# Warm products of 128 columns, expert weights rounded later, and an earlier finish of a tile, in a conditioned mixture-of-experts block

## What is computed

```
h  = einsum('bct,bcd->bdt', x, table[conditions])        # 4096 rows of 256
u  = square(relu(h @ up_w))                              # 256 -> 1024
m  = (h @ expert_weight) * top_2(h @ gate_w).sum()       # 256 -> 256, one scale per row
y  = u @ down_w + m                                      # 1024 -> 256
out = x + (y - mean(y)) * rsqrt(var(y) + 1e-5) * gamma + beta
```

## Time and profile before

| what | value |
|---|---|
| median of 3 runs (lowest, highest) | 230.84 us (230.8, 231.0) |
| the profiled execution's own time | 230.09 us |
| its span, first to last instruction | 228.5 us |
| TensorE busy with products, with weight loads | 221.8 us (97%), 191.9 us (84%) |
| VectorE, ScalarE, GpSimd busy | 162.2, 105.7, 130.5 us |
| granted TensorE clock over the span | 1.00 |
| stores of the last block's tiles | 4 of 128 KB, 1.7 us from issue to landing |

### The profile page before, as it was taken

One profiled execution on the slowest core, in us unless ns is written; L12 is line 12 of the kernel. 1 busy time (PEld: TensorE's weight loads), 2 busy tenths in 40 slices (PEclk: granted clock), 3 DMA queues, 4 the chain that ended last, 5 costly groups with the idle time before them and its releaser, 6 DMA issues.

```text
span 228.5 us, 3998 instructions
## 1 busy us (share of the span) xinstructions
PE 221.8 (97%) x1260; PEld 191.9 (84%) x1260; DVE 162.2 (71%) x352; ACT 105.7 (46%) x187; POOL 130.5 (57%) x131
## 2 busy tenths in 40 slices
PE   7999999999999999999999999999999999999992
PEld 2888888988898888888888888888888888888892
DVE  6486975877667877667677766587766766777884
ACT  3378944444455355444545435534454444444000
POOL 3748776575536663656555664366555575557411
PEclk9999999999999999999999999999999999999999
DMA  3867123030503011000200002000020002000021
GB/s 98 239 205 227 41 68 102 8 99 7 185 11 98 9 43 53 0 0 3 92 0 0 3 0 95 0 3 0 0 95 1 0 0 71 25 0 0 19 99 69
DMA packets 17177, 11.81 MB, mean 52 GB/s; under 512 B 6660, under 2 KB 16900, under 8 KB 17156
## 3 DMA queue, kind: packets, MB, share of 16 engines
q1 hardware_dynamic: 15460, 10.43, 15.2%
q10 hardware_dynamic: 1280, 1.07, 1.5%
q0 software_dynamic: 416, 0.05, 0.2%
HBM read 7.35 MB, written 4.19 MB: 51 GB/s over the span
## 4 chain that ended last, share of the span: by engine, by line
PE 93%; DVE 2%; DMA 1%; issue 1%; ACTq 1%; ACT 0%; DVEq 0%
PE up_ps L337 38%; PE down_ps L431 25%; PE down_ps L433 13%; PE hid_ps L303 5%; PE moe_ps L447 3%; PE moe_ps L449 3%; PE moe_ps L448 3%; DMA wd<-in_L_cond_weights_dram 1%; ACTq L513 1%; PE down_ps L303 1%; DVE up_lo L619 1%; DMA cond_row<-in_itok_B_dram 1%; PE down_ps L429 0%; PE down_ps L427 0%; PE down_ps L428 0%
## 5 line engine op out<-in xcount | busy, mean ns | idle before, releaser
L677 POOL TENSOR_TENSOR sq_lo<-square,sq_hi 128x512 fp32r<-128x512 f32 x64 | 83.6, 1310 | 78.6 <-DVE square L552 77.4
L431 PE MATMUL down_ps<-down_hl,sq_hi 128*128 128x512 f32 x248 | 88.8, 393 | 0.0
L433 PE MATMUL down_ps<-down_hl,sq_lo 128*128 128x256 f32 x248 | 69.6, 280 | 0.0
L552 DVE SCALAR_TENSOR_TENSOR square<-up_ps,relu 128x512 f32<-128x512 f32 x64 | 43.8, 686 | 35.7 <-ACT relu L491 26.2
L431 PEld LDWEIGHTS down_ps<-down_hl,sq_hi 128*128 128x128 f32 x248 | 46.5, 188 | 10.8 <-issue 0.3
L491 ACT ACTIVATE relu<-up_ps 128x512 f32<-128x512 f32 x64 | 38.1, 595 | 33.5 <-PE up_ps L337 33.5
L337 PE MATMUL up_ps<-hid_hi,up_hi 128*128 128x512 f32 (+1 forms) x136 | 52.8, 391 | 0.7 <-ACT hid_hi L476 0.3
L337 PE MATMUL up_ps<-hid_hi,up_lo 128*128 128x512 f32 (+1 forms) x136 | 51.1, 379 | 0.0
L433 PEld LDWEIGHTS down_ps<-down_hl,sq_lo 128*128 128x128 f32 x248 | 46.7, 188 | 2.4
L493 ACT ACTIVATE sq_hi<-relu 128x512 fp32r<-128x512 f32 x64 | 40.5, 633 | 2.0
L337 PE MATMUL up_ps<-hid_lo,up_hi 128*128 128x512 f32 (+1 forms) x136 | 40.6, 381 | 0.0
(11 more groups left out here) (62 smaller groups left out, 195.6 us busy)
## 6 DMA issues: line engine op xcount, KB each, us to landing
x_sb<-in_x_dram SPq DMA_DIRECT2D x7, 512.0 KB, 4.3
out_dram<-result SPq DMA_DIRECT2D x7, 512.0 KB, 3.1
wd<-in_L_cond_weights_dram SPq DMA_DIRECT2D x111, 4.0 KB, 1.6
x_sb<-in_L_ffn_down_w_dram SPq DMA_DIRECT2D x2, 512.0 KB, 4.4
x_sb<-in_x_dram ACTq DMA_DIRECT2D x2, 256.0 KB, 3.0
result<-in_L_ffn_up_w_dram ACTq DMA_DIRECT2D x2, 256.0 KB, 2.9
result<-in_L_ffn_up_w_dram SPq DMA_DIRECT2D x1, 512.0 KB, 4.6
out_dram<-result SPq DMA_DIRECT2D x4, 128.0 KB, 1.7
```

Of the source, the lines that this page charges most:

```text
L431: pe.matmul(dst[:, :], a_hi, down_hl[:, c, :, :].rearrange("p s t -> p (s t)"), start=(c == 0), stop=False)
L433: mm = pe.matmul(dst[:, T:2 * T], a_lo, down_hl[:, c, 0, :], start=False, stop=(c == CH - 1))
L552: dve.scalar_tensor_tensor(square[:, c % 2, :], up_ps[c % UPB][:, :], 0.0, relu[:, c % 2, :], ALU.max, ALU.mult).then_inc(square_done, 1)
L677: pool.tensor_tensor(sq_lo[:, j % 2, c, :], square[:, c % 2, :], sq_hi[:, j % 2, c, :].bitcast(f32), ALU.subtract).then_inc(sq_lo_done, 1)
```

## The change

Three things are changed. The warm products become 42 products of 128 columns, whose operands are both the program's constant one; the tile `warm`, its fill and the wait for it go. The rounding of the expert and gate weights moves on ACT behind `rectify(0, 0)`, and its low part on DVE behind `square_up(0, 0)`. In the last block, tile 2 is finished right behind tile 1, ahead of the work on tile 3.

```
-WARM = 10
+WARM = 42
...
-            pe.wait_ge(warm_ready, 1)
+            one = nc.const_aps.tensor(1.0, [P, P], bf16)
             for _ in range(WARM):
-                pe.matmul(up_ps[0][:, :], warm[:, 0:P], warm[:, :], start=True, stop=True)
+                pe.matmul(up_ps[0][:, 0:P], one, one, start=True, stop=True)
...
             hidden_first(1, 1)                                      # ACT
-            act.wait_ge(eg_landed, 32)
-            act.activation(eg_hi[:, :, :], eg_raw[:, :, :], ACT.Copy).then_inc(eg_hi_ready, 1)
...
                     rectify(j, c)
+                    if j == 0 and c == 0:
+                        act.wait_ge(eg_landed, 32)
+                        act.activation(eg_hi[:, :, :], eg_raw[:, :, :], ACT.Copy).then_inc(eg_hi_ready, 1)
...
-            dve.memset(warm[:, :], 1.0).then_inc(warm_ready, 1)
...
             split_up(2)                                             # DVE
-            dve.wait_ge(eg_hi_ready, 1)
-            dve.tensor_tensor(eg_lo[:, :, :], eg_raw[:, :, :], eg_hi[:, :, :].bitcast(f32), ALU.subtract) \
-                .then_inc(eg_lo_ready, 1)
...
                         square_up(j, c)
+                    if j == 0 and c == 0:
+                        dve.wait_ge(eg_hi_ready, 1)
+                        dve.tensor_tensor(eg_lo[:, :, :], eg_raw[:, :, :], eg_hi[:, :, :].bitcast(f32), ALU.subtract) \
+                            .then_inc(eg_lo_ready, 1)
...
                         if block < BLOCKS - 1:
                             finish(block, t)
-                        elif t > 0:
+                        elif 0 < t < TILES - 1:
                             finish(block, t - 1)
+                            if t == TILES - 2:
+                                finish(block, t)
```

More of the change, by code:

```diff
@@ L70, in adaln_ffn @@
         table_loaded = sb("table_loaded", [P, 1])
-        warm = sb("warm", [P, 512], bf16)
         hid_hi = sb("hid_hi", [P, 2, K, TOK], f32r)
@@ L120, in adaln_ffn @@
         result_moved = [sem("result_moved_even"), sem("result_moved_odd")]
-        warm_ready, consts_ready = map(sem, ("warm_ready", "consts_ready"))
+        consts_ready = sem("consts_ready")
         wd_zeroed = [sem("wd_zeroed_block0"), sem("wd_zeroed_rest")]
```

## The result

The changed kernel is slower: 231.18 us at the median of 9 runs (230.28 to 231.79) against 230.80 for the kernel before (9 runs, 230.11 to 231.0). The ratio is 1.0032, 95% interval 1.002 to 1.0045; the ratios here are worked out from the single times and are not the quotients of the medians. I had forecast 230.2.

What follows compares the result with a forecast made beforehand. PE's stream was taken as the bound (93% of the chain of waits). Gains of 0 + 0.48 + 0.10 + 0.05 = 0.63 us from the median 230.84 gave 230.2 us, own range 230.0 to 230.4, with rivals 229.5 to 230.9.

Steps and rivals of the forecast that it cites:

- The warm part is thus worth 0 to the end: Start: 42 products at 0.11 us end at 5.7, hidden because group 1's matrix holds PE until 6.80; gain 0.
- Rival 2: Start: weight loads pace the small warm products at 0.22 us each, 2.0 us late; time 232.2; chance 7%.
- the pace of 0.162: Start: load-and-product pairs at the lower clock, 0.162 us each, would end the warm products at 7.9, 1.5 past the cover.
- SP waits for none of the moved work, so this stays: Block 1's conditioning: SP's last matrix still lands at 16.57, leaving 0.48 us of the 0.56 gained.
- The expert weights, 0.48 us: Chunk 0's square comes earlier, PE's wait before 14.99 goes, and 0.48 us reaches the end; bounds 0 to 0.56.
- From then on PE doesn't wait in either trace: After block 1's conditioning, from about 16.6 us: no new PE wait, so the 0.48 us gain is kept.
- Hidden, with 0.8 to spare: eg_lo on DVE, 14.4 to 15.1 us, is ready 0.8 us before PE's expert products at 15.9.
- The finish: Tail: last finish starts 0.65 us after POOL's power, gaining 0.10; the last store running alone gains 0.05.
- Rival 1: Block 1's matrices land 0.3 us later and decide; total gain 0.15 to 0.4, time 230.6; chance 17%.
- Rival 3: Clock rises later, 1.5 to 2 us into the dense stretch from 7.86; 0.75 to 1.0 lost, net 231.2; 5%.
- Rival 4: Start 0.54 us earlier brings the clock's rise forward, some 0.5 to 0.7 us on top; 229.6; chance 9%.

Runs made afterwards that it cites:

- warm_only: Kernel before with only the warm products changed to 42 of 128 columns on the constant one; 231.51 against 230.44 us, ratio 1.0040.
- experts_only: Kernel before with only the rounding of the expert weights moved; 230.74 against 230.44 us, ratio 1.0006.
- finish_only: Kernel before with only tile 2 of the last block finished earlier; 230.35 against 230.44 us, ratio 0.9997.
- all_10x512_pool_waits: Whole change, but ten warm products of 512 columns on the constant one, and POOL's first sq_lo waits for eg_lo; 230.39 against 230.41 us, ratio 1.0004.
- const_10x512: Kernel before with its ten 512-column warm products on the constant one, without the fill; 230.42 against 230.41 us, ratio 0.9999.
- all_gate: all_10x512_pool_waits with DVE's gate for block 0's tile 2 moved ahead of squares 8 and 9; 230.27 against 230.37 us for the kernel before, ratio 1.0013.
- const_84x64: Kernel before with 84 warm products of 64 columns on the constant one; 231.65 against 230.44 us, ratio 1.0075.
- const_32x160: Kernel before with 32 warm products of 160 columns on the constant one; 230.32 against 230.44 us, ratio 1.0003.

## Why the prediction was wrong

- **The step that failed:** "The warm part is thus worth 0 to the end". Its own working held: 0.107 us a product against my 0.11, the matrix of group 1 at 6.67 against 6.80, no cost up to 7.86. But I counted the added instructions as columns and not as instructions. They cost 1.07 us at the median (warm_only), by a way that none of my rivals had: the fetch at 13.7 instead of 21.5 us, SP's issue of 1.45 instead of 0.42, the down weights' landing at 18.96 instead of 17.57, ACT, the expert products at 32.66 instead of 31.62. That the place of the fetch is the cause rests on these traces and on the table of widths, with the open ends said there. Rival 2, pacing by the weight loads, was of the right sign for the wrong reason; the 0.107 us refutes it, and with it the pace of 0.162 that I had scaled from the 81 ns of the Trainium skill, "TensorE: Matmul & The Clock Gate", section "Back-to-back issue gap".
- **"SP waits for none of the moved work, so this stays":** no semaphore, but SP's issue itself took 1.0 us longer (of the down weights in the profile after, of a matrix of block 1 in warm_only).
- **The expert weights, 0.48 us:** with this part the wait for the square went in eight of nine traces, and chunk 4 began at 14.5 to 14.9 in seven of them, 0.1 to 0.5 earlier (at 15.13, with 0.2 of the wait left, where the up weights landed late, and at 15.97 where the clock had fallen). "From then on PE doesn't wait in either trace" was the false sentence. A view that shows no wait doesn't show the slack. It was 0.16 us at 31.6 and less than nothing at 39.7, where the view of PE's weight loads of the kernel before already has a wait for ACT's scaled result (0.3 us) that I didn't use. DVE, ACT and POOL set the time of block 0 and 1, and the moved work stayed in their stream.
- **"Hidden, with 0.8 to spare":** I looked at when eg_lo is needed and not at who runs beside it. It moved from a place where POOL idled to one 0.05 to 0.25 us from POOL's first operation, and in experts_only PE did wait 0.3 us for it.
- **The finish:** start 0.65 behind POOL's power and 0.1 gained, as worked out; from there to the span's end 2.7 us instead of 2.8, within the 0 to 0.1 of the store. By itself (finish_only) the part isn't told apart from nothing.
- **Rival 1**, the matrices of block 1: they held PE in all_10x512_pool_waits and for up to 0.2 us after, but decided nothing, since the later waits were the tighter ones. **Rival 3**, a later clock, didn't show in the profile after (products of 256 columns 0.12 us apart from 7.92 on); a clock that fell again did in other kernels, see the last section. **Rival 4** didn't show: the same median in eleven runs of const_10x512, which starts just as early.
- **The median that I subtracted from** (230.84, three runs) was itself 0.4 us above what the kernel before showed later. Had the whole gain come, the time would have been near 229.8, and not the 230.2 of the forecast.

## What to carry to other kernels

Count added instructions also as bytes to be fetched, and look where in the DMA view the fetches of the engine stand: a piece that moves into a burst of loads can hold up the engine that issues them. Before crediting a removed wait to the end, walk PE's later semaphores and subtract, for each, the producer's end from the consumer's start; the smallest difference is all that can be gained. Work that is moved between two engines has a neighbour on the other engine, too.

## What the hardware showed unexpectedly

- The first fetch of 16 KB of instructions took 1.06 us of one DMA engine (1.0 to 1.1 in the 19 traces), and it stretched one DMA issue of SP from 0.3 to 0.5 us to 1.0 to 1.5 us, in the burst and behind it, in 18 of 19 traces. It stood at 11 to 14 us or at 20.1 to 21.8 us and nowhere between.
- DVE's operations on SBUF operands can stretch while POOL runs its own: 0.70 to 1.82 us for eg_lo, 0.48 to 1.45 for a finish, and 0.69 to 1.79 for the down weights' low part. Where eg_lo began first, POOL's sq_lo stretched instead, 1.29 to 1.82. DVE's squares, which have one operand in PSUM, stayed at 0.69 in all these traces.
- The granted clock can fall again after it rose. In the profiled execution of all_gate (231.64) PE stood idle for 0.63 us before 6.74 and once more before 7.79; from 8 to 11 us the clock was at 0.50, 1.2 GHz, and products of 256 columns came 0.21 us apart. Windows: length, busy PE, PEld, DVE, ACT, POOL, clock, DMA share, GB/s.

```profile
7.00:8.00 1.00, 0.66 (x6) 0.50 (x6) 0.32 (x1) 0.69 (x3) 0.68 (x2) 1.00 0.99 335
8.00:9.00 1.00, 1.00 (x6) 1.00 (x6) 0.81 (x3) 0.59 (x1) 0.84 (x3) 0.50 0.70 94
```

Its second conditioning began at 11.17 instead of 9.90 us (all_10x512_pool_waits), and its time is 1.25 us above that one's. Idle pieces alone don't decide it: all_10x512_pool_waits stood idle longer (0.91 before 5.64, 0.54 before 6.86), and its clock stayed at 1.00. But the mean clock listed for each timed execution shows a pattern. Of the 77 executions of kernels whose warm products start at 0.95 us on the constant, nine have 0.993 or less: four of all_gate, three of const_84x64, one each of all_10x512_pool_waits and const_32x160, and all nine took 231.6 us or more (to 233.3). Of the 240 with the filled tile for which it is listed none is under 0.995. So the earlier start carries a risk of its own. The nine of the changed kernel don't show it, and which of the differences in the start brings it isn't shown.
